# A graph network of six message passes: edge groups without holes, and consumers that walk pairs of group and tile

## The chip, the cores and the metric

The kernel runs on one core of a Trainium2 chip. The metric is the device time of one execution in microseconds (us). Three runs of the kernel before gave a median of 14,485.1 us, from 14,473.6 to 14,488.4. The core's engines have instruction queues of their own: TensorE (PE, its weight loads PEld), VectorE (DVE), ScalarE (ACT), GpSimd (POOL) and SyncE (SP). They meet through semaphores.

## The reference

There are 6,250 nodes with 64 features and 200,000 edges (src, dst), sorted by dst, with a weight, 16 attributes and 8 attributes each. After a layer norm and a ReLU each of four blocks adds its result to x:

```
L0: 3 times  agg[dst] += weight * ht[src]            (hyperbolic layers, 64 features)
L1: e = leaky_relu(er[dst] + el[src] + attributes16 . v);  softmax of e over the edges of a dst;
    h[dst] += alpha * xt[src];  then a layer norm
L2: h[dst] += relu(A[src] + B[dst] + attributes8 @ E) @ W2
L3: as L1, without attributes, with another slope
```

These are six passes over all edges: three GCN passes (n = 0, 1, 2), attention (n = 3), MLP (n = 4), attention (n = 5).

## The kernel before

**Groups and tiles.** The nodes are T = 49 tiles of 128. A group is 256 edges, two columns of 128, and all edges of a group point into one tile. The kernel sorts the edges itself: it counts them by tile, gives each tile a whole number of groups (the last one of a tile has holes), and computes where each edge goes. The number of groups must hold for any distribution, so NG = 832, in ITER = 52 iterations of BODY = 16 groups. A table `sched` gives the tile of each group; it goes through DRAM into one partition, and PE and DVE load 24 of its words into registers at the head of each iteration (`tiles_of`).

**Before the passes.** DVE computes positions in chunks (`PLACED`), SP brings slabs of the payload, and POOL scatters them with 1,568 indirect DMAs (line 450) into `packed` in DRAM, 32 words an edge. `packed` has been filled with harmless values before that, by 42 DMAs of SP. Then SP reads `packed` back, 16 columns at a time in two buffers, and DVE unpacks them (`unpack`, line 1167) into W, DL, SRC, EAV and EA8. Three iterations are unpacked ahead, the others within the first pass.

**A pass.** A node table goes to DRAM. SP copies 16 indices at a time from SRC to `idx`; POOL gathers the rows of the source nodes, one indirect DMA for a column of 128 edges (line 469), into G, which has room for 16 groups. A gather of group q waits until group q of the iteration before is used. Semaphores are one for each place q in the ring, and consumers wait for `gathered[..][q]` (`need_rows`). In a GCN pass only 28 of 32 columns come so; the last four are chosen on PE from a copy of the table on the chip: DVE makes one-hots of each of the 49 tiles (`tile_hots`, line 788), PE multiplies (line 1559), DVE takes the sums into G (`take_rows`). The MLP pass does that for two columns, attention for none.

**The consumers** go through the groups in order. GCN: DVE makes a weighted one-hot of the destinations (line 749), PE multiplies it with G (line 1534), DVE adds the result to ACC at the group's tile (line 924). Attention is a chain of some 13 small DVE instructions a group (own scores line 768, maximum 838 to 845, shift 859 to 865, exponents 873 to 881, one-hot 760, weighing 887, adding up 930), with transposes and products on PE and one-hots and exponentials on ACT. MLP: line 896 adds the gathered row to what PE computed, then ReLU and a split in three bf16 parts, line 927 adds up. All loops over iterations are hardware loops whose bodies are unrolled over the 16 groups; each engine walks its own in program order.

Of the kernel before, what the change touches and what calls it, by code (L numbers as in the profile page):

```python
# [23 lines left out]
P = 128  # L24
# [13 lines left out]
NG = -(-((N_EDGES + T * (GE - 1)) // GE) // BODY) * BODY  # L38
PLACED = [2, 3, 5, 9, 15, 15]
ACT_BINS = 28  # L40
PACK = 40
NS = 1680
# [4 lines left out]
ROW = D + 1  # L47
ITER = NG // BODY
PASSES = 6
PIECE = BODY  # L50
AHEAD = 3
# [13 lines left out]

assert STEPS_N % 2 == 1 and 2 * ITER * PIECE == 2 * NG
assert max(PLACED) * 2 * SLAB <= 512 and sum(PLACED) * 2 * SLAB == KC and NS % PACK == 0 and (NS // PACK) % 2 == 0 and KC % (2 * SLAB) == 0
assert NS * P >= NG * GE + P * KC - N_EDGES + GE and P * SCHED >= NG + BODY

# [33 lines left out]
def build(nc, d, out):  # L103
    with ExitStack() as ctx:
# [17 lines left out]
        W = sb("W", [P, NS])  # L122
        DL = sb("DL", [P, NS])
        SRC = sb("SRC", [P, 2 * NG + 2 * BODY], I32)
        EAV = sb("EAV", [P, NS])
        EA8 = sb("EA8", [P, NS, D8])

        ea8_flat = EA8[:, :, :].rearrange("p s c -> p (s c)")
        bucket, mask, signs, rank = (ea8_flat[:, i * KC:(i + 1) * KC] for i in range(4))
        signs = signs.bitcast(BF16).rearrange("p (h c) -> p h c", h=2)  # L130
        dst_raw = ea8_flat[:, 5 * KC:6 * KC].bitcast(I32)
        pos = ea8_flat[:, 6 * KC:7 * KC].bitcast(I32)
        pos_hi = ea8_flat[:, 7 * KC:8 * KC].bitcast(I32)
# [8 lines left out]
        fill = y_flat[:, 0:PACK * PAY].rearrange("p (s c) -> p s c", c=PAY)  # L142
        slab = y_flat[:, PACK * PAY:PACK * PAY + 2 * SLAB * PAY].rearrange("p (h s c) -> p h s c", h=2, c=PAY)
# [4 lines left out]
        grp_i = sb("grp_i", [P, NB], I32)  # L148
        sums = sb("sums", [P, NB])
        before = U[:, :, :].rearrange("p t c -> p (t c)")[:, 0:SCHED * T].rearrange("p (j t) -> p j t", t=T)  # L150
        sched_f = sb("sched_f", [P, SCHED])
        sched_i = sb("sched_i", [P, SCHED], I32)
        sched = sb("sched", [1, P * SCHED + LAG], I32)
# [35 lines left out]
        G = sb("G", [P, 2 * BODY, ROW])  # L189
# [73 lines left out]
        packed = nc.dram_tensor("packed", (P, NS, PAY), F32).ap()  # L263
        packed_rows = packed.rearrange("p s c -> (p s) c")
        table = nc.dram_tensor("table", (P * TP, ROW), F32).ap()
        sched_d = nc.dram_tensor("sched_d", (P * SCHED,), I32).ap()
# [4 lines left out]
        fill_made, filled = sem("fill_made"), sem("filled")  # L271
# [48 lines left out]
        def landed(n):  # L320

            return 32 * ITER * LANDS[:n].count(LANDS[n])
# [5 lines left out]
        def steps(eng, body, lag):  # L328


            for u in range(BODY):
                body(u, 0)
            with nc.Fori(1, ITER, engines=[eng.engine], hint_back_edge=True) as i:
                body(None, i)
            for u in range(lag):
                body(u, ITER)
# [8 lines left out]
        def _(sp):  # L345
# [20 lines left out]
            sp.wait_ge(fill_made, 1)  # L366
# [5 lines left out]
            sp.wait_ge(fill_made, 2)  # L372
            for k in range(NS // PACK):
                sp.dma_start(packed[:, k * PACK:(k + 1) * PACK, :], fill).then_inc(filled, 16)

            sp.wait_ge(sched_made, 2)
            sp.dma_start(sched_d.rearrange("(p j) -> p j", p=P), sched_i[:, :]).then_inc(sched_stored, 16)
            sp.wait_ge(sched_stored, 16)
            sp.dma_start(sched[0:1, LAG:LAG + P * SCHED], sched_d.rearrange("(a n) -> a n", a=1)).then_inc(sched_loaded, 16)
# [14 lines left out]
            for h in range(2):  # L394
                sp.wait_ge(scattered[h], KC // (2 * SLAB) * 16 * SLAB)
            sp.wait_ge(first_rows, 1)

            def fetch(j):

                for h in range(2):  # L400
                    if not isinstance(j, int) or j > 0:
                        sp.wait_ge(unpacked, j * 2 + h)
                    sp.dma_start(pack_buf[h], packed[:, ds((j * 2 + h) * PIECE, PIECE), :]).then_inc(pack_in[h], 16)
# [1397 lines left out]
```

## Time and profile before

The profiled execution of the kernel before has a span of 14,473.0 us from its first to its last instruction; the median of the runs, 14,485.1 us, is 12.1 us above it.

| | PE | PEld | DVE | ACT | POOL |
|---|---|---|---|---|---|
| busy, us | 9,746.3 | 8,816.7 | 10,317.1 | 5,084.8 | 10,529.2 |
| share of the span | 67% | 61% | 71% | 35% | 73% |

The chain of waits that ended last goes by engine: PE 39%, issue 18%, DVE 16%, POOL 14%, DVE's queue 8%, ACT 3%, DMA 2%. The first 2,213 us are setup and scatters. The passes then take, from one boundary to the next, about 1,895, 1,875, 1,858, 2,166, 2,012 and 2,121 us.

An engine's busy time is what its instructions cover; instructions of a queue alone (register operations, waits, loads of registers) are shown as DVEq, PEq, SPq and are not in it. "Issue" is time for which the profile shows no wait. In a list of one line's instructions the three durations are minimum, median and maximum in ns, then come the first and the last start.

### The profile page before, as it was taken

To read this page: it belongs to the slowest core of one execution; us is meant where nothing else is said; L and a number is where in the kernel's file an instruction comes from. 1 tells how busy PE (TensorE), PEld (TensorE's weight loads), DVE (VectorE), ACT (ScalarE), POOL (GpSimd) and SP (SyncE) were. 2 spreads that over 40 slices of the span, in tenths; PEclk is the share of its full clock that TensorE was granted. 3 is DMA by queue.
4 is the path that set the end of the run, shared out by engine and by line. 5 is a ranking of instruction groups with operands and counts; after the bars stand their busy time and mean duration, and the time that the engine had idled before them with its cause. 6 is when DMAs were issued, how large, how long until landed. Compare 5 with 4: busy or idle time off the path is not lost.

```text
span 14473.0 us, 400585 instructions
## 1 busy us (share of the span) xinstructions
PE 9746.3 (67%) x94470; PEld 8816.7 (61%) x94471; DVE 10317.1 (71%) x47961; ACT 5084.8 (35%) x16333; POOL 10529.2 (73%) x10828
## 2 busy tenths in 40 slices
PE   0000006777778888788887788888577777888888
PEld 0000006777767777677777677777455555777777
DVE  7870007777776666666666888888888887888888
ACT  1000000000000000000000788888577676777777
POOL 3777777777767777677777677777577776677776
PEclk9995557888888888888888555555788888555555
DMA  2101112222211111111111111111111111111111
GB/s 101 26 25 26 26 26 47 41 41 41 40 27 27 27 27 27 27 27 27 27 27 25 30 28 27 27 27 27 23 26 26 26 26 24 30 28 28 28 28 30
DMA packets 496417, 441.99 MB, mean 31 GB/s; under 512 B 289869, under 2 KB 315085, under 8 KB 494926
## 3 DMA queue, kind: packets, MB, share of 16 engines
q0 software_dynamic: 346368, 334.42, 13.9%
q1 hardware_dynamic: 149454, 102.38, 2.5%
q14 instruction: 556, 4.55, 0.1%
q8 instruction: 39, 0.64, 0.0%
HBM read 364.93 MB, written 65.20 MB: 30 GB/s over the span
## 4 chain that ended last, share of the span: by engine, by line
PE 39%; issue 18%; DVE 16%; POOL 14%; DVEq 8%; ACT 3%; DMA 2%; ACTq 0%; POOLq 0%; SPq 0%
PE bank L1559 16%; PE bank L1534 11%; POOL packed L450 9%; POOL G L469 4%; DVEq L732 4%; PE bank L1616 3%; PE bank L1628 3%; DMA G<-table,idx 2%; DVE OH L749 2%; PE bank L1605 1%; PE bank L1718 1%; PE bank L1547 1%; DVEq L734 1%; PE bank L1632 1%; DVE OHT L788 1%
## 5 line engine op out<-in xcount | busy, mean ns | idle before, releaser
L469 POOL DMA_INDIRECT G<-table,idx x9256 | 9007.0, 973 | 3237.1 <-issue 2497.9
L1452 ACT ACTIVATE OHB<-bank,const 128x512 bf16<-128x512 f32 x159 | 109.2, 687 | 6718.5 <-PE bank L1547 6718.5
L1559 PE MATMUL bank<-UZ,OHT 128*128 128x192 bf16 x15600 | 2093.5, 261 | 543.5 <-DVE OHT L788 543.5
L1534 PE MATMUL bank<-G,OH 128*128 128x64 f32 x9984 | 1683.9, 300 | 589.0 <-DVE OH L749 449.6
L450 POOL DMA_INDIRECT packed<-Y,slab_pos x1568 | 1522.0, 971 | 671.5 <-issue 495.4
L1559 PE MATMUL bank<-UZ,V 128*128 128x192 bf16 x14976 | 1994.0, 259 | 0.0
L1534 PEld LDWEIGHTS bank<-G,OH 128*128 128x128 f32 x9984 | 1494.1, 217 | 760.2 <-DVE OH L749 678.6
L1559 PEld LDWEIGHTS bank<-UZ,OHT 128*128 128x128 bf16 x15600 | 1511.1, 111 | 583.0 <-DVE OHT L788 561.4
L1534 PE MATMUL bank<-ZR,OH 128*128 128x65 f32 x6656 | 1765.4, 419 | 1.8 <-DVE ZR L887 1.8
L1534 PEld LDWEIGHTS bank<-ZR,OH 128*128 128x128 f32 x6656 | 1623.8, 334 | 2.1 <-DVE ZR L887 2.0
L749 DVE TENSOR_SCALAR OH<-const,DL,W 128x128 f32<-128x128 f32 x4992 | 1560.6, 367 | 0.2 <-issue 0.2
L924 DVE TENSOR_TENSOR ACC<-ACC,bank 128x64 f32 x2496 | 550.0, 220 | 1241.4 <-PE bank L1534 1203.9
L788 DVE TENSOR_SCALAR OHT<-OHB 128x512 bf16<-128x512 bf16 x3900 | 1157.7, 297 | 388.1 <-issue 386.8
L1559 PEld LDWEIGHTS bank<-UZ,V 128*128 128x128 bf16 x14976 | 1408.1, 104 | 16.0
L1628 PE MATMUL bank<-ER,OHT 128*128 x9984 | 1001.4, 174 | 505.0 <-DVE negm_lo L865 310.4
L1628 PEld LDWEIGHTS bank<-ER,OHT 128*128 128x128 bf16 x9984 | 783.8, 105 | 786.8 <-issue 617.8
L1616 PE MATMUL bank<-const,V 128*128 128x128 f32 x3328 | 1117.9, 440 | 57.7 <-ACT V L1391 49.9
L788 DVE TENSOR_SCALAR V<-OHB 128x512 bf16<-128x512 bf16 x3744 | 1143.5, 305 | 0.0
L1547 PE MATMUL bank<-const,chosen 128*128 128x128 f32 x1272 | 222.6, 330 | 1293.1 <-DVE chosen L524 1293.1
L760 DVE TENSOR_TENSOR OHB<-iota_b,DLw 128x256 bf16<-128x256 bf16 x2496 | 1046.8, 419 | 21.6 <-issue 12.6
L1547 PEld LDWEIGHTS bank<-const,chosen 128*128 128x128 f32 x1272 | 195.5, 233 | 1293.7 <-DVE chosen L524 1293.7
L1605 PE MATMUL bank<-ident_b,OHB 128*128 128x128 bf16 x4992 | 942.9, 286 | 19.0 <-DVE OHB L760 19.0
(303 smaller groups left out, 21034.3 us busy)
## 6 DMA issues: line engine op xcount, KB each, us to landing
G<-table,idx POOLq DMA_INDIRECT x9256, 2.5
packed<-Y SPq DMA_DIRECT2D x42, 640.0 KB, 17.7
UZ<-packed SPq DMA_DIRECT2D x104, 256.0 KB, 2.7
Y<-in_payload SPq DMA_DIRECT2D x98, 256.0 KB
packed<-Y,slab_pos POOLq DMA_INDIRECT x1568
table<-Y SPq DMA_DIRECT2D x6, 1690.0 KB, 5.5
idx<-SRC SPq DMA_DIRECT2D x624, 8.0 KB
X<-in_x SPq DMA_DIRECT2D x1, 1568.0 KB, 8.0
```

The lines of the kernel that those rows point to most:

```text
L450: pool.indirect_dma_start(out=packed_rows, out_offset=bass.IndirectOffsetOnAxis(ap=slab_pos[:, h, c:c + 1], axis=0), in_=slab[:, h, c, :], ...
L469: pool.indirect_dma_start(out=G[:, 2 * q + c, :], out_offset=None, in_=table, in_offset=bass.IndirectOffsetOnAxis(ap=idx[:, h, j:j + 1], a ...
L732: v.load(tregs, sched[0:1, bass.ds(i * BODY, BODY + LAG)] if not isinstance(i, int) else sched[0:1, i * BODY:(i + 1) * BODY + LAG])
L749: o = v.tensor_scalar(OH[:, q, c, :], iota, DL[:, at], W[:, at], ALU.is_equal, ALU.mult)
L760: v.tensor_tensor(OHB[:, q, :, :], iota_b[:, :].unsqueeze(1).to_broadcast([P, 2, P]), DLw[:, 2 * u:2 * u + 2].unsqueeze(2).to_broadcast([P ...
L788: v.tensor_scalar(tile_hot(tile), code, float(tile), None, ALU.is_equal).then_inc(tile_ready, 1)
L1534: o = pe.matmul(ps_a[r % 2][:, 0:w], OH[:, q, c, :], parts[c], start=c == 0, stop=c == 1)
L1547: o = pe.matmul(ps_code[:, c * P:(c + 1) * P], chosen[:, c:c + 1].to_broadcast([P, P]), ident, start=True, stop=True)
L1559: o = pe.matmul(ps_rows[c // 2][:, c % 2 * 3 * D:(c % 2 + 1) * 3 * D], tile_hot(tile)[:, c * P:(c + 1) * P], table_parts[:, tile, :, :].re ...
L1605: o = pe.matmul(ps_m[r % 2][:, c * P:(c + 1) * P], OHB[:, q, c, :], ident_b[:, :], start=True, stop=True)
L1616: o = pe.transpose(ps_x[r % 2][:, c * P:(c + 1) * P], V[:, r % 4, c, :], ident)
L1628: pe.matmul(e[:, c:c + 1], one, ER3[:, bass.ds(t, 1), k], start=k == 0, stop=k == 2)
```

## The change

The edges are packed without holes. Group g is edges 256 g to 256 g + 255 of the order by dst, so there are NGR = 784 groups in NCH = 49 iterations of gathers. A group may now touch several tiles. The consumers walk a list of *pairs* (group, tile); there can be 782 + 48 of them, and the list is still NG = 832 long, ITER = 52 iterations. For an edge of another tile than the pair's the local destination lies outside 0..127: no one-hot matches it, and a mask adds a very low score in attention. The table `sched` has four rows (tile, group, first pair of a group, and tile and column together); `quads` holds the group of each fourth pair. G is a ring of RING = 4 iterations, 64 groups, and POOL's loop is unrolled over the four.

Consumers no longer wait on the semaphore of a place. SP waits for each gather in order and counts `rows_here`; a consumer waits every fourth pair until `rows_here` has reached the group of a pair some steps on, a value that it has in a register. The column in G comes out of a register too. The fill of `packed` is gone; `packed` is read back by pairs, each a DMA of two columns, on ACT's queue in the first pass; the 8 attributes go through a table in DRAM (`e8_items`) and come back in the MLP pass; the indices are brought from the order of pairs to that of groups by 16 DMAs an iteration. The table-row work on the chip is done in the first 49 iterations alone.

```diff
+NGR = KC // 2
+NCH = NGR // BODY
-NG = -(-((N_EDGES + T * (GE - 1)) // GE) // BODY) * BODY
+NG = -(-(-(-N_EDGES // GE) + T - 1) // BODY) * BODY
+RING = 4
-AHEAD = 3
+AHEAD = 5
...
+        def values(eng, what, n, top):
+            loads[0] += 1
+            regs = [eng.alloc_register(f"v{loads[0]}_{j}") for j in range(n)]
+            eng.load(regs, what)
+            return [eng.snap(r, donate=True, min_val=0, max_val=top) for r in regs]
+        def items_of(eng, row, i, back, top):
+            return values(eng, sched[0:1, row, ds(i * BODY + (LAG - back), BODY + back)], BODY + back, top)
+        def quads_of(eng, i):
+            return values(eng, quads[0:1, ds(i * (BODY // 4), BODY // 4 + 1)], BODY // 4 + 1, NGR - 1)
+        def need_rows(eng, n, quad, u, i):
+            if u % 4 == 2 or (u == 0 and isinstance(i, int)):
+                eng.wait_ge(rows_here, (quad[(u + 2) // 4 if u else 0] & 1023) + (n * NGR + 1))
...
+                def rows_of(i, last):                                  # SP, in each pass
+                    for h in range(2):
+                        end = min(BODY // 2 * (h + 1), fetched(n))
+                        for q in range(BODY // 2 * h, end):
+                            sp.wait_ge(gathered[LANDS[n]][q], i * 32 + (landed(n) + 32))
+                            sp.sem_inc(rows_here, 1)
+                        if not last:
+                            indices(i + 1, h)
+                    for q in range(fetched(n), BODY):
+                        ...
+                        sp.sem_inc(rows_here, 1)
...
-                gathers(0)
-                with pool.Fori(1, ITER) as i:
-                    gathers(i)
+                gathers(0, 0)
+                with pool.Fori(0, NCH // RING) as i:
+                    for k in range(RING):
+                        gathers(i * RING + (k + 1), (k + 1) % RING)
...
-                    need_rows(g, q)
-                    v.tensor_tensor(EL[:, r, :], G[:, 2 * q:2 * q + 2, D], EAV[:, bass.ds(g * 2, 2)],
+                    need_rows(v, n, quad, u, i)
+                    v.tensor_tensor(EL[:, r, :], G[:, bass.ds(col, 2), D], (EAV if n == 3 else MASK)[:, ds(g * 2, 2)],
...
-                    v.tensor_tensor(ZR[:, r % 4, :, 0:D], G[:, 2 * q:2 * q + 2, 0:D],
+                    v.tensor_tensor(ZR[:, r % 4, :, 0:D], G_wide[:, bass.ds(col, 2), 0:D],
...
-                        if live(0) and n == 3:
-                            own_scores(g, u, u % 8)
+                        if live(0):
+                            own_scores(g, u, i, u % 8, cols[u + LAG], quad)
...
-                        sums(g, u % 8, u % 2, n, [G[:, 2 * u + c, 0:D] for c in range(2)], D)
+                        sums(g, u % 8, u % 2, n, [G[:, bass.ds(body.cols[u] + c, 1), 0:D].rearrange("p a c -> p (a c)")
+                                                  for c in range(2)], D)
...
+                    own.count(v.tensor_scalar(MASK[:, at], DL[:, at], 0.0, None, ALU.is_lt))      # in unpack
+                    stt(MASK[:, at], DL[:, at], float(P - 1), MASK[:, at], ALU.is_gt, ALU.add)
+                    ts(MASK[:, at], MASK[:, at], NO_SCORE, None, ALU.mult)
+                    tt(EAV[:, at], EAV[:, at], MASK[:, at], ALU.add)
...
+                def each(i, fetching):                                 # ACT, in the first pass
+                    a.wait_ge(unpacked, (i + AHEAD) * 2 + 3)
+                    if fetching:
+                        fetch(i + AHEAD + 1)                           # 16 DMAs of two columns
+                    to_groups(i + 2)                                   # 16 DMAs of SRCI to SRC
+                    code_made(0, i + 1)
+                    if fetching:
+                        store_e8(i + AHEAD + 1)                        # 2 DMAs
```

## Rows read from the trace of the kernel before

**Rows 1.** Windows of four passes: length, then PE, PEld, DVE, ACT, POOL busy.

```profile
4155.00:6030.00 1875.00, 1539.00 (x14040) 1448.98 (x14040) 1258.33 (x5205) 47.80 (x104) 1411.77 (x1451) 0.85 0.17 26
...
7995.00:10161.00 2166.00, 1862.44 (x16640) 1649.14 (x16640) 1784.30 (x10923) 1764.94 (x5826) 1595.01 (x1664) 0.50 0.17 28
...
10265.00:12277.00 2012.00, 1457.59 (x18616) 1161.53 (x18616) 1628.61 (x8319) 1415.57 (x4211) 1532.23 (x1551) 0.82 0.16 26
...
12330.00:14451.00 2121.00, 1847.09 (x16640) 1660.38 (x16640) 1788.01 (x10091) 1660.80 (x5825) 1596.80 (x1664) 0.50 0.17 28
```

**Rows 2.** The gathers, line 469, in the windows of passes 1, 3, 4, 5.

```profile
L469 POOL DMA_INDIRECT G<-table,idx x1451: 940/944/1381, 4154.8 to 6007.7; - x182
...
L469 POOL DMA_INDIRECT G<-table,idx x1664: 938/944/1197, 8000.6 to 10127.3; - x185
...
L469 POOL DMA_INDIRECT G<-table,idx x1551: 940/944/1493, 10265.0 to 12268.6; - x194
...
L469 POOL DMA_INDIRECT G<-table,idx x1664: 940/944/1196, 12334.4 to 14437.1; - x185
```

**Rows 3.** Timeline of POOL in pass 1: start, duration, idle before.

```profile
5012.53 0.94 POOL L469 DMA_INDIRECT G<-table,idx  x1 [0.30 <-issue]
```

**Rows 4.** DVE once a group: line 924 in pass 0, line 873 in 3, 5.

```profile
L924 DVEq FUSED_REGOPS  x832: 57/65/70, 2238.0 to 4091.6; - x167
...
L873 DVE TENSOR_TENSOR e_u<-EL,bank x832: 142/149/158, 8014.5 to 10157.8; 128x2 f32<-128x2 f32 x167
L873 DVE TENSOR_TENSOR e_u<-G,bank x832: 142/149/158, 12345.5 to 14447.6; 128x2 f32<-128x2 f32 x167
```

**Rows 5.** Timeline of DVE in pass 3, one step.

```profile
9002.18 0.15 DVE L873 TENSOR_TENSOR e_u<-EL,bank 128x2 f32<-128x2 f32 x1
...
9004.38 0.15 DVE L873 TENSOR_TENSOR e_u<-EL,bank 128x2 f32<-128x2 f32 x1
```

**Rows 6.** Timeline of DVE in pass 0, one half of an unpack.

```profile
3015.74 0.18 DVE L524 TENSOR_SCALAR W<-UZ 128x16 f32 x1 [0.36 <-issue]
...
3017.22 0.16 DVE L1184 TENSOR_SCALAR itmp<-UZ 128x16 int32<-128x16 int32 x1
3017.51 0.18 DVE L1187 SCALAR_TENSOR_TENSOR SRC<-itmp 128x16 int32 x1
3017.83 0.17 DVE L524 TENSOR_SCALAR W<-UZ 128x16 f32 x1
```

**Rows 7.** Chain of waits at the head of an iteration, pass 1: start, us.

```profile
5011.13 1.60 DVEq L732
...
5012.76 0.23 DVEq L734
...
5013.02 0.17 DVEq L734
```

**Rows 8.** Chain of waits in pass 3, within one step.

```profile
9003.18 0.04 DVEq L864
...
9003.48 0.23 issue
...
9004.07 0.08 DVEq L768
```

**Rows 9.** Timeline of PE in pass 1: one sum to the next.

```profile
5023.06 0.58 PE L1534 MATMUL bank<-G,OH 128*128 128x64 f32 x4
...
5024.80 0.58 PE L1534 MATMUL bank<-G,OH 128*128 128x64 f32 x4
```

**Rows 10.** Timeline of POOL: the first scatter and the first gather.

```profile
157.41 1.12 POOL L450 DMA_INDIRECT packed<-Y,slab_pos  x1 [156.95 <-DMA slab_pos<-EA]
...
2220.47 1.44 POOL L469 DMA_INDIRECT G<-table,idx  x1 [26.56 <-DMA idx<-SRC]
```

**Rows 11.** Timeline of SP: two DMAs of a slab.

```profile
1503.09 0.34 SPq L391 DMA_DIRECT2D Y<-in_payload  x1
1503.57 0.50 SPq L392 DMA_DIRECT2D slab_pos<-EA  x1
```

More of the change, by code:

```diff
@@ L47 @@
 ROW = D + 1
+RING = 4
+COLS = RING * 2 * BODY
 ITER = NG // BODY
@@ L392, in _ @@
                         sp.dma_start(slab_pos[:, h, :], pos[:, bass.ds(at, SLAB)]).then_inc(slab_in[h], 16)
[L394 to L403, printed above, removed]
-            for j in range(AHEAD):
-                fetch(j)
-            sp.wait_ge(unpacked, 2 * AHEAD + 1)
             for n in range(PASSES):
@@ L1441, in body @@
                                 tiles(i + 1, 0)
+                a.wait_ge(quads_made, 1)
+                for h in range(2):
+                    a.wait_ge(e8_out[h], 16 * ITER)
+                load_e8(0)
                 codes(0)
                 tiles(0, 0)
-                steps(a, body, 1)
-            def codes(n):
-                def made(i):
-                    a.wait_ge(code_spread, i + (n * (ITER + 1) + 1))
-                    need(a, tile_ready, i * T + n * ITER * T)
-                    a.activation(code, ps_code[:, 0:ON_CHIP * P], ACT.Identity, bias=own_row).then_inc(code_ready, 1)
-                made(0)
-                with a.Fori(1, ITER + 1) as i:
-                    made(i)
+                for u in range(BODY):
+                    body(u, 0, True)
@@ new lines, in mlp_pass, with code_made @@
+                with nc.Fori(1, NCH, engines=[a.engine], hint_back_edge=True) as i:
+                    body(None, i, True)
+                with nc.Fori(NCH, ITER - 1, engines=[a.engine], hint_back_edge=True) as i:
+                    body(None, i, False)
+                for u in range(BODY):
+                    body(u, ITER - 1, False, last=True)
+                body(0, ITER, False, last=True)
+            def code_made(n, i):
+                a.wait_ge(code_spread, i + (n * (NCH + 1) + 1))
+                need(a, tile_ready, i * T + n * NCH * T)
+                a.activation(code, ps_code[:, 0:ON_CHIP * P], ACT.Identity, bias=own_row).then_inc(code_ready, 1)
@@ L1722, in mlp_pass @@
                 spread_e(0)
-                steps(pe, with_tiles(step), 6)
+                steps(pe, with_tiles(step), 6, on_chip=True)
             pe.wait_ge(sched_loaded, 16)
-            tregs = [pe.alloc_register(f"tile{j}") for j in range(BODY + LAG)]
             pe.wait_ge(blocks_made, 2)
```

485 lines of the change are left out of this document (291 added, 194 removed).

## The prediction

> **What bounds the kernel now.** I read the table by stretch first, because six passes, n = 0 to 5, with different limits fill 12,200 of the 14,473 us. [rows 1]: GCN passes of about 1,870 us (n = 1 is shown), attention passes of 2,166 and 2,121 us, the MLP pass of 2,012 us. In each the engine with the most regular work is POOL, which issues the gathers. Its list of starts [rows 2] gives the pace: 1,456 gathers (1,451 recorded) in 1,853 us in pass 1, 1.273 us each, so 28 x 1.273 = 35.7 us an iteration; 30 gathers in 38.6 us in the MLP pass; 32 in 40.9 and 40.5 us in the attention passes. The median gather takes 0.944 us, and 0.30 us of issue lie before the next [rows 3]; a few longer ones make up the rest, so in GCN and MLP the queue of gathers never rests: it is the bound, though the chain of waits mostly names PE and DVE.
>
> Next the pace of the consumers [rows 4]: 16 groups take 16/831 of the time from first to last. That is 35.7 us in pass 0, 41.3 and 40.5 in the attention passes. In attention I then read single steps of DVE [rows 5]: from one e_u to the next is 2.20 us in the middle of an iteration, and in it the instructions start one behind the other without a gap. 16 such steps and the head of an iteration, with its table load, are the 41.3 us. So attention has two bounds within 1%: POOL and DVE. Fewer gathers can lower only one of them. PE is third: at a granted clock of 0.50 it is busy 1,862 of 2,166 us [rows 1], 35.8 of 41.7 an iteration.
>
> **The arithmetic of the change.** The edges are 200,000/256 = 782 groups, padded to 784 = 49 iterations; before, they were 832 = 52. But the list of pairs has 782 + 48 = 830 entries, padded to 832. So the gathers, and the choice of rows from the on-chip table, drop by 3 iterations of 52 a pass; every step of the consumers (one-hots, sums, scores, adding up) is still made 832 times, and now finds its column by a register.
>
> **Step 1, GCN passes 1 and 2.** Removed: 3 x 35.7 = 107 us of gathers a pass. What is late next: the consumers. Groups arrive for 49 x 35.7 us and must serve 52 iterations of pairs, so the consumers have 33.6 us for 16 pairs. What they need can be read from pass 0, where DVE also unpacks two halves of 2.1 us [rows 6] and hardly waits: 35.7 - 4.2 = 31.5 us, at most. The change adds on DVE a load of 5 registers and four waits on a register's value. The load of 24 takes 1.60 us and the two copies behind it 0.23 + 0.17 [rows 7]. Between those ends, one fifth of 1.60 (0.33) and 1.60, I take 0.95; the copies go, as the registers are now donated: +0.5 net. A wait with its register instruction is 0.04 to 0.08 and 0.05 before the next [rows 8]: 4 x 0.15 = 0.6, half of it hidden where PE paces at 1.74 us a pair [rows 9]. PE must compute two addresses a pair: 0 (run ahead, behind 16 matmuls) to 0.2 us (both bare), so 0 to 3.2 us an iteration; I take 0.9. Its new load of 16 registers lies beside DVE's, during which PE waits. In all 31.5 + 0.5 + 0.3 + 0.9 = 33.2 us, just under 33.6. I take -100 us for each pass, -200, with -107 and -20 as ends of one.
>
> The Trainium skill (DMA: Bandwidth & Descriptors, Latency and other measured facts) gives a register load a floor of about 600 ns; an estimate by it, 0.6 plus 5/24 of the remaining 1.0, is 0.8 us instead of my 0.95, which would change an attention pass by 8 us. No run shows a short load yet.
>
> **Step 2, the MLP pass.** 3 x 38.6 = 116 us of gathers go. DVE, busy 1,629 of 2,012 us [rows 1] or 31.3 an iteration, keeps POOL's pace now; it gains the 0.4 us of copies and pays a column for `hidden`, 16 x 0.1 = 1.6 us, on a need that I put near 35 us (31.3 and the 3.7 that a head of an iteration takes without work). The wait for rows goes to ACT, which is busy 1,416 of 2,012 us [rows 1]; behind it queue the transposed one-hots, and ACT also issues one 64 KB load of attributes an iteration. Taken: -108 (ends -116 and -40).
>
> **Step 3, attention.** No gather that is saved helps, since DVE sets 41.3 us. Queued behind its new wait, in own_scores, is its whole instruction stream; V on ACT and the shift wait for that. Added per pair: own_scores and weigh address G by a register (decode, multiply, base), the tile number is decoded twice, and one wait in four pairs. The chain shows the address of EAV in one fused register instruction, 0.08 us, between L841 and L768, bare [rows 8]; two or three more operations there cost about 0.05. The window of 0.23 us before ZR (behind the reduction L838) hides weigh's. Decoding the tile adds about 0.02. Sum 0.08 us a pair; ends 0 (all hidden) and 0.35 (four register instructions of 0.04 with their 0.05, all bare). So 16 x 0.08 = 1.3, +0.5 load, +0.6 waits, -0.3 of waiting for rows that goes: 2.1 us, times 52 = +109 us (ends +20 and +330) for pass 3. Pass 5 had no own_scores: the two differ by 41.3 - 40.5 = 0.8 us an iteration. 0.8 + 2.1 = 2.9 us, and the pace before was 40.5: +151 us (ends +60 and +370).
>
> A rule that speaks for this price: the Trainium skill (Vector Engine (DVE) Microarchitecture Reference, Instruction fetch and dispatch) says that every DVE instruction passes through the full dispatch, register instructions too. The trace agrees in so far as these take 0.04 to 0.08 us of DVE's queue each [rows 8], with 0.05 to the next.
>
> **Step 4, before and in pass 0.** The schedule needs some 25 more small DVE operations ahead of the first positions, on the path to the first scatter at 157.4 us [rows 10]: about +8, less 1 for the fill that goes. The fill's writes are over long before and return nothing. The start: now POOL rests 26.6 us between the last scatter and the first gather at 2,220.5 [rows 10]. Now ACT must fetch by groups, 16 DMAs where there were 2. One on SP took 0.34 us, with a register on an SBUF side 0.50 [rows 11]; ends on ACT 0.3 and 1.0, taken 0.5. A round is 16 issues, 8 us, and some 4 us of landing and of the first half of an unpack, 12 us; SRC of the first iteration needs the fourth round and 16 more DMAs, so gathers start near 2,263. DVE's further unpacks lie in that wait: consumers start 39 us later. The iteration: unpack has 12 operations a half, not 9, three or four of them dependent, 0.29 us from one to the next (L1184 to L1187) [rows 6]: +1.9. With the half microsecond of load, 0.2 of waits and 0.5 for PE, less 0.9 of waiting for rows: 35.7 + 2.2 = 37.9 us. 47 x 37.9 + 2 x 33 + 3 x 20 (no table rows) = 1,907 against 1,856: +51. Pass and start +90 (ends -60 and +220). ACT's queue then holds 34 DMAs, about 25 us of 38, so the code it also makes is in time.
>
> **Sum.** 7 + 90 - 200 - 108 + 109 + 151 = +49 us on the profiled execution's 14,473.0, which becomes 14,522. The median of the runs, 14,485.1, lies 12 us above that span; so 14,535 us.
>
> **The rivals.**
> A, the queue has room: DVE's register work is hidden and the load is short. Attention +25 and +65, MLP -112, GCN -107 each, pass 0 with its start +50, setup +7: -179 us, 14,306. For it: gaps of 0.23 us in the step; against it: only one such gap in 2.20 us.
> B, decoding is not fused: four bare register instructions a pair, 0.35 us. Attention +310 and +350, pass 0 +180, MLP -50, GCN -50 each, +7: +697, 15,182. Also a halfway case. Against it: the address of EAV is one fused instruction, 0.08 us.
> C, pass 0 becomes bound by ACT: 34 DMAs at 1.0 us and the register loads make about 43 us, and the code for the table rows, queued behind them, comes late. From 0.75 us a DMA this decides. 46 x 5 = +230 over my sum, 14,765. By the Trainium skill (DMA: Bandwidth & Descriptors, Specifications) pieces under 512 B are not moved at line rate; here they are 256, 32 and 8 B. That would lengthen landings, of which five iterations of lead hide 100 us.
> D, the consumers in GCN need over 34.4 us for 16 pairs, PE's addresses bare: GCN gains 20, not 100: +160, 14,695.
>
> **How the numbers follow.** Forecast 0.45, A 0.27, B (with its halfway case) 0.10, C 0.08, D 0.10. The range 14,300 to 14,830 holds A, the forecast, C and D, and leaves out some 2 in 10; the forecast's own is 14,440 to 14,640. Runs of this kernel tell about 0.2%, 29 us, from no change. Faster is A and a tenth of chance out of the forecast's lower end: 0.36; same 0.14; slower 0.50.
>
> **What would show it.** 1,372 gathers in passes 1 and 2, at 1.27 us, and these passes near 1,770 us; DVE waiting for rows seldom there. Attention: e_u to e_u in mid-iteration 2.25 to 2.30 us, 43.4 us an iteration in both passes, POOL with gaps over 0.30 us. The short TENSOR_LOAD near 0.95 us. Pass 0: heads of iterations 2 us longer, ACT DMAs near 0.5 us, first gather near 2,270. I am wrong if attention's step stays at 2.20 us (A), if it goes beyond 2.4 (B), or if pass 0 has DVE waiting on ACT's code (C).

## The result: 2.8% slower, and where the time went

The kernel after the change takes 14,897.6 us (median of 4 runs, 14,886.2 to 14,902.6), the kernel before 14,486.8 us (4 runs, 14,473.6 to 14,494.9): a ratio of 1.028, interval 1.0267 to 1.0296. The prediction, 14,535 with 14,300 to 14,830 as its range, is too low by 363 us. Slower was right; the size of one step, attention, was not, and pass 0 had the wrong sign.

In the profiled execution (span 14,884.4 us, of before 14,473.0) I took the stretches one after the other, each from its first to its last add-up of a sum, and set them beside the terms of the prediction:

```
stretch                           before    after   change   predicted
up to the first add-up of n = 0   2238.2   2331.9    +93.7   +7 and (with the pass) +90
n = 0, GCN                        1853.5   1802.0    -51.5
n = 1, GCN                        1854.6   1751.6   -103.0   -100
n = 2, GCN                        1854.6   1757.8    -96.8   -100
n = 3, attention                  2138.7   2403.2   +264.5   +109
n = 4, MLP                        1994.9   1874.5   -120.4   -108
n = 5, attention                  2096.4   2503.3   +406.9   +151
between passes, end                                  +18         0
```

The windows of the same four passes as in [rows 1] (length, then PE, PEld, DVE, ACT, POOL busy, PEclk), the answer of the kernel after:

```profile
4200.00:5956.00 1756.00, 1391.34 (x13324) 1351.88 (x13323) 1207.15 (x5039) 34.05 (x50) 1327.55 (x1365) 0.85 0.17 26
7870.00:10278.00 2408.00, 1897.17 (x16570) 1646.53 (x16570) 1854.65 (x10874) 1690.97 (x5799) 1461.64 (x1547) 0.50 0.14 23
10394.00:12273.00 1879.00, 1426.67 (x18232) 1141.63 (x18231) 1628.05 (x8200) 1353.43 (x4038) 1421.88 (x1451) 0.84 0.18 30
12356.00:14865.00 2509.00, 1889.98 (x16562) 1653.44 (x16562) 1946.18 (x10877) 1691.21 (x5793) 1461.21 (x1546) 0.50 0.13 22
```

Pass 3 is 242 us longer than in [rows 1], and DVE's busy time in it grew by only 70: what was added is not vector work. The gathers, answering to [rows 2], by pass (count, durations, first and last start):

```profile
L518 POOL DMA_INDIRECT scratch<-table,idx x1372: 940/944/3357, 4186.9 to 5942.3; - x196
L518 POOL DMA_INDIRECT scratch<-table,idx x1568: 938/944/1146, 7843.2 to 10096.1; - x196
L518 POOL DMA_INDIRECT scratch<-table,idx x1470: 940/945/4784, 10355.6 to 12256.8; - x184
L518 POOL DMA_INDIRECT scratch<-table,idx x1568: 938/942/1187, 12328.3 to 14674.9; - x196
```

In GCN and MLP one starts every 1.28 and 1.29 us, as before, and there are 84 and 90 fewer: the gain is their number. In attention one starts every 1.44 and 1.50 us: POOL waits now, and the last add-up comes 180 and 187 us after the last gather. The group's step on DVE, as in [rows 4] and [rows 5]: e_u by pass, then from one e_u to the next.

```profile
L935 DVE TENSOR_TENSOR e_u<-EL,bank x830: 142/149/158, 7865.9 to 10266.5; 128x2 f32<-128x2 f32 x166
L935 DVE TENSOR_TENSOR e_u<-EL,bank x832: 142/149/158, 12348.8 to 14857.5; 128x2 f32<-128x2 f32 x167
```

```profile
9018.63 0.15 DVE L935 TENSOR_TENSOR e_u<-EL,bank 128x2 f32<-128x2 f32 x1
9021.11 0.15 DVE L935 TENSOR_TENSOR e_u<-EL,bank 128x2 f32<-128x2 f32 x1
```

A plain step (by that I mean the length from one e_u to the next that stands most often in the pass) takes 2.48 us where it took 2.20; in pass 5 it is 2.63 where it was 2.16, and the median of all its steps is 2.79. The chain of waits through own_scores shows what came in, where [rows 8] had one fused instruction of 0.08 us:

```profile
9015.18 0.04 DVEq L836
9015.22 0.03 issue
9015.26 0.10 DVEq L836
9015.36 0.03 issue
9015.39 0.05 DVEq L836
9015.44 0.05 issue
9015.49 0.07 DVE EL L836
```

The first is the mask that takes the column out of the register (ALU_OP), the other two are the addresses of G and of EAV (FUSED_REGOPS). So a mask is an instruction of its own; so is each address; and each has an issue of 0.03 to 0.08 us behind it. The same holds at the sums: the line of add_up has now two register instructions a pair, where it had one fused one of 0.064:

```profile
L991 DVEq ALU_OP  x1664: 40/45/50, 7872.2 to 14862.0; - x185
L991 DVEq FUSED_REGOPS  x1664: 98/106/113, 7872.2 to 14862.1; - x185
```

The loads (the short one had no row before; [rows 7] had the long one and its copies, which are gone):

```profile
L384 DVEq TENSOR_LOAD <-sched x318: 1598/1604/1864, 2317.0 to 14846.8; - x159
L384 DVEq TENSOR_LOAD <-quads x260: 590/595/616, 2318.9 to 14801.0; - x130
L384 ACTq TENSOR_LOAD <-quads x52: 534/538/562, 10378.2 to 12226.3; - x52
```

And the start, answering to [rows 10]: the first scatter, the last scatters, the first gather on POOL.

```profile
177.29 1.12 POOL L499 DMA_INDIRECT packed<-Y,slab_pos  x1 [176.83 <-DMA slab_pos<-scratch]
...
2226.41 0.96 POOL L499 DMA_INDIRECT packed<-Y,slab_pos  x1 [0.31 <-issue]
2305.31 0.97 POOL L518 DMA_INDIRECT scratch<-table,idx  x1 [77.94 <-DMA idx<-SRC]
```

### The profile page after: what moved, and what is told of

Read it like the earlier page. It is cut to its first block, busy times and chain, and to the rows that moved or that the text cites. A ratio compares the mean times of both kernels' runs of the same rounds, so it can differ in the third digit from the quotient of the medians.

```text
span 14884.4 us, 423582 instructions
## 1 busy us (share of the span) xinstructions
PE 9489.7 (64%) x92328; PEld 8592.3 (58%) x92329; DVE 10563.2 (71%) x48623; ACT 5003.6 (34%) x16178; POOL 10002.6 (67%) x10294
## 4 chain that ended last, share of the span: by engine, by line
issue 23%; PE 22%; POOL 19%; DVE 18%; DVEq 11%; ACT 4%; DMA 2%; ACTq 1%; POOLq 0%; SPq 0%
PE bank L1720 11%; POOL packed L499 10%; POOL scratch L518 9%; PE bank L1698 5%; DVEq L384 4%; DVE ZR L949 2%; DMA scratch<-table,idx 2%; DVEq L836 2%; DVE OHB L828 1%; DVE negm_lo L927 1%; PE bank L1771 1%; PE bank L1783 1%; PE bank L1873 1%; DVE r_rest L924 1%; ACT OHT L1440 1%
## 5 line engine op out<-in xcount | busy, mean ns | idle before, releaser
L518 POOL DMA_INDIRECT scratch<-table,idx x8722 | 8466.6, 971 | 3981.8 <-issue 2525.2
L1720 PE MATMUL bank<-UZ,OHT 128*128 128x192 bf16 x14700 | 1979.2, 262 | 702.1 <-DVE OHT L858 702.1
L1698 PE MATMUL bank<-scratch,OH 128*128 x9984 | 1638.1, 295 | 521.5 <-DVE ACC L985 322.7
L1720 PE MATMUL bank<-UZ,V 128*128 128x192 bf16 x14112 | 1890.2, 260 | 0.0
L1720 PEld LDWEIGHTS bank<-UZ,OHT 128*128 128x128 bf16 x14700 | 1429.6, 111 | 738.6 <-DVE OHT L858 715.8
L1698 PEld LDWEIGHTS bank<-scratch,OH 128*128 128x128 f32 x9984 | 1476.8, 214 | 581.6 <-issue 570.6
L1720 PEld LDWEIGHTS bank<-UZ,V 128*128 128x128 bf16 x14112 | 1332.7, 105 | 15.9
L1466 ACT ACTIVATE V<-OHB,EL 128x128 f32<-128x128 bf16 x3328 | 1153.4, 393 | 518.0 <-DVE EL L836 415.3
L858 DVE TENSOR_SCALAR V<-OHB 128x512 bf16<-128x512 bf16 x3528 | 1058.3, 300 | 0.0
L1708 PE MATMUL bank<-const,chosen 128*128 128x128 f32 x1200 | 170.9, 286 | 1295.4 <-DVE chosen L574 1295.4
```

What stands on the lines that cost most here:

```text
L518: pool.indirect_dma_start(out=G[:, slot * 2 * BODY + 2 * q + c, :], out_offset=None, in_=table, in_offset=bass.IndirectOffsetOnAxis(ap=idx ...
L858: v.tensor_scalar(tile_hot(tile), code, float(tile), None, ALU.is_equal).then_inc(tile_ready, 1)
L1466: o = a.activation(V[:, r % 4, c, :], OHB[:, q, c, :], ACT.Identity, scale=-BIG, bias=EL[:, r, c:c + 1])
L1698: o = pe.matmul(ps_a[r % 2][:, 0:w], OH[:, q, c, :], parts[c], start=c == 0, stop=c == 1)
L1720: o = pe.matmul(ps_rows[c // 2][:, c % 2 * 3 * D:(c % 2 + 1) * 3 * D], tile_hot(tile)[:, c * P:(c + 1) * P], table_parts[:, tile, :, :].re ...
```

## The experiments

The theory after the result (T): attention pays for register instructions in DVE's queue. Against it stood: a cost of the packed layout itself, waiting for the count of arrived groups, and register work that lies hidden. A place is the number of an instruction in the iteration. Times are medians; the interval is that of the ratio to the kernel before, run beside it on the same chip.

**pairs_in_attention.** Everything of the change stays in GCN and MLP; attention gathers by pairs again.

```
- sp: idx <- SRC (by groups), NCH rounds
+ sp, n in (3, 5): idx <- SRCI (by pairs), ITER rounds; pool: G[:, 2q + c, :], fixed
- G[:, bass.ds(col, 2), ...]; need_rows out of quads; own_scores in both passes
+ G[:, 2 * q:2 * q + 2, ...]; wait_ge(gathered[1][u], i * 32 + ...); own_scores in n = 3 only
```

> The changed kernel, but both attention passes (n = 3, 5) gather by pairs again: 832 x 2 gathers with fixed columns of G out of the unpacked list SRCI, no table of columns, no waits out of a table, no own_scores in pass 5 (its scores are read straight from G as before). GCN and MLP stay packed. The theory (T): the loss of attention is register work in VectorE's queue, so pass 3 goes from 2,403 back to about 2,140 us (first to last add-up) and pass 5 from 2,503 to about 2,095, while passes 0, 1, 2 and 4 keep 1,802, 1,752, 1,758 and 1,875: 14,898 - 264 - 407 = about 14,225 us, a ratio to the kernel before of 0.982. The rival (R): the loss comes with the packed layout itself (G inside the large scratch tile, a ring of 64 groups, lists changed) or with the boundaries, and then attention stays over 2,250 us a pass and the kernel over 14,480.

Measured: 14,171.5 us, ratio 0.979 (0.9772 to 0.9805), faster than both. e_u in the two passes:

```profile
L966 DVE TENSOR_TENSOR e_u<-EL,bank x832: 142/149/158, 7861.6 to 9968.8; 128x2 f32<-128x2 f32 x167
L966 DVE TENSOR_TENSOR e_u<-scratch,bank x832: 142/149/159, 12043.5 to 14139.2; 128x2 f32<-128x2 f32 x167
```

Pass 3 takes 2,102 us from first to last add-up, pass 5 2,093, with G still inside the large tile: the layout costs nothing that shows, and the whole loss of attention belongs to how consumers find and await their rows and tiles and, in pass 5, to own_scores, which went too. Pass 3 is even 37 us shorter than before; the reason comes below. These 37, and 16 us less between the passes, make up the 54 by which the kernel is under my 14,225.

**before_one_mask.** In the kernel before, add_up masks its tile's register.

```
+ if att: t = t & 63
  acc = ACC[:, bass.ds(t, 1), :]
```

> The kernel before, with one more register instruction a pair on VectorE in both attention passes: add_up masks the register of its tile (t & 63, which changes nothing) ahead of the address. The price of one bare register instruction. T: 0.04 and 0.05 to the next, 0.09 us x 832 x 2 = +150 us at most, 14,635, ratio 1.010; less where part of it falls into a stall of the step. Rival A: 0. As fused in the prediction's step 3 (0.02 a pair): +33 us, ratio 1.002.

Measured: 14,569.8 us, ratio 1.006 (1.0047 to 1.0081), +90 us. That lies between the 150 of T and the 33 of fused work, but it is no price of a mask: in pass 3 a plain step went from 2.21 to 2.25 and the pass became shorter, 2,100 us, while pass 5 took 2,217 (+120), with steps of 2.24 instead of 2.16. The chain at the head of an iteration of pass 5 has what the sum did not (the branch is line 333):

```profile
12507.60 0.07 DVEq L333
12507.66 2.05 issue
12509.71 0.04 DVEq L333
```

The same place in pass 5 of the kernel before:

```profile
12534.88 0.07 DVEq L333
12534.95 0.46 issue
12535.41 0.04 DVEq L333
```

1.6 us an iteration, 84 us a pass, behind the branch, where nothing was changed but the 16 more instructions in each attention loop. This gave theory L, the position of the code.

**before_addresses.** Meant to add the addresses of G as well.

```
+ col = v.snap(t & 64, min_val=0, max_val=1) + 2 * q     # in weigh and own_scores
```

> The kernel before, with the register work of the change added to VectorE in both attention passes and nothing else of it: weigh and (in pass 3) own_scores find their column of G by a register (one mask of the tile's register, which gives 0, and the address from it), add_up masks its tile. Same gathers, same waits, same results. T: pass 3 gains 0.25 us a pair (three masks of 0.04 with their 0.05, not all of the address hidden), 0.20 to 0.28: 832 x 0.25 = +208; pass 5, without own_scores, 0.17 (0.09 to 0.20): +141; together +350 us, 14,835, ratio 1.024. The rival (A as in the prediction: register work is hidden in the gaps of the step): under +50 us, ratio under 1.004.

Measured: 14,560.8 us, ratio 1.0055 (1.0038 to 1.0071). Its trace has the same instructions as before_one_mask: the address, being 0 by its bounds, was folded away. It is a second measurement of one mask, and says nothing on the addresses.

**wait_by_pair.** No table for the wait.

```
- if u % 4 == 2 ...: eng.wait_ge(rows_here, (quad[...] & 1023) + (n * NGR + 1))
+ if PLAN[n][0] == ATT and u % 4 == 0: eng.wait_ge(rows_here, i * BODY + (n * NGR + u + 4))
```

> The changed kernel, in attention only the wait for rows is changed: every fourth pair waits on the count of arrived groups against a value made of the loop's counter (16 i + u + 4), later than needed, instead of one out of the table; the load of 5 registers and the masks of that value go. T: an iteration loses the 0.6 us of the short load and of four times 0.36 us some 0.23 each, 1.5 us in all, 52 x 1.5 = 78 us a pass, 14,898 - 156 = about 14,740 us. The rival (W, consumers really wait for arrivals, counted by SP): waiting for a group up to 48 groups later than the one needed makes the passes longer, over 14,950 us. If neither the load nor the masks are on the path: 14,900.

Measured: 14,912.3 us, ratio 1.0299 (1.0282 to 1.0316). Pass 3 fell from 2,403 to 2,353 us, pass 5 rose from 2,503 to 2,573: its gap behind the branch is 2.3 us where the kernel after has 0.52. Without that (1.8 x 52 = 94) pass 5 would be 24 us shorter. The total stands where I had put it for a load and masks that are not on the path (14,900), but by two changes that cancel. The rival W fails: pass 3 became shorter though it waits for later groups. The register work of the wait costs 1.0 us an iteration in pass 3, less than the 1.5 expected. The steps of 3.02 us that held the wait are gone from pass 3, but some of 2.82 to 2.88 stand there, about 0.36 above the plain 2.49: by the size, gaps of the kind that pairs_shifted shows below.

**static_columns, twice.** The addresses of G go. Own_scores and weigh read fixed rows of Y in their place, so this kernel leaves the gathered rows out of attention's sums; gathers, waits and masks of the tile stay.

```
- G[:, bass.ds(col, 2), D]                 (own_scores)
+ Y[:, 2 * u:2 * u + 2, D]
- G_wide[:, bass.ds(col, 2), 0:D]          (weigh)
+ Y[:, 2 * r:2 * r + 2, 0:D]
```

> The changed kernel, in attention only: own_scores and weigh read two fixed rows of Y (the table's source, not written during a pass) instead of the two columns of G that a register names. It leaves the gathered rows out of attention's arithmetic; gathers, waits, masks of the tile and everything else stay. It prices the addresses of G. The theory in its present form (N: attention pays per instruction put into VectorE's queue, about 0.058 us each, 5.09 us an iteration for 86 instructions in pass 3 and 7.84 for 135 in pass 5): four register instructions and one fused one go from the step, so the step falls from 2.49 to about 2.30 us in pass 3 and from 2.55-2.63 to about 2.40 in pass 5; 16 x 0.2 = 3.2 us an iteration, 166 us a pass, about 14,570 us, give or take 90 us for the code's position (theory L below). Rival (the addresses lie hidden beside vector work, and the masks of the tile and the waits are the price): under 0.05 us a pair, over 14,820 us.

This run, pairs_shifted and early_start fell on a chip on which the kernel before takes 19,835 us, not 14,480. They gave 19,952 (ratio 1.005, 1.003 to 1.007), 20,020 (1.009, 1.0066 to 1.0106) and 19,982 us (1.008, 1.006 to 1.0093): on that chip packing GCN and MLP shows no gain either. I had put its state down to PE standing still; in its trace of static_columns PE does so for up to 4.3 us between 11,300 and 11,420 us, but in the same stretch of the second time for up to 4.8, so that is not what sets the chip apart. What does stays open. All three were run again on another.

> The kernel static_columns once more, on another chip. The first time the kernel before itself took 19,835 us, and the trace of this kernel shows PE standing still for 2 to 3.7 us some twice in 145 of its instructions (11,300 to 11,420 us) and 28 gathers in 47 us: a state of that chip in which attention is bound by PE's stream, so that its ratio, 1.005, says nothing on VectorE's. Expected on a chip where the kernel before takes 14,480 us, as written then: N 14,570 us (step of pass 3 at 2.30 us, of pass 5 at 2.40), 90 us either way for the code's position; rival over 14,820 us with steps within 0.05 us of 2.49 and 2.63.

Measured: 14,583.0 us, ratio 1.0075 (1.0058 to 1.0092). e_u by pass:

```profile
L935 DVE TENSOR_TENSOR e_u<-EL,bank x832: 142/149/158, 7869.5 to 10121.7; 128x2 f32<-128x2 f32 x167
L935 DVE TENSOR_TENSOR e_u<-EL,bank x832: 142/149/158, 12197.6 to 14560.0; 128x2 f32<-128x2 f32 x167
```

A plain step takes 2.28 us in pass 3 and 2.44 in pass 5 (expected 2.30 and 2.40; the medians of all steps are 2.45 and 2.61), the passes are 156 and 146 us shorter, the kernel 315. The addresses of G are three fifths of attention's loss in pass 3, a third in pass 5; the rival (hidden addresses) is out. In the chain above it is own_scores' address that stands bare; weigh's mask and address (L949, 0.045 and 0.057 us) run beside a reduction of 0.42 us.

**pairs_own_scores.** pairs_in_attention, but with the masked scores kept in pass 5, on fixed columns.

```
- if live(0) and n == 3: own_scores(...)
+ if live(0): own_scores(...)        # EL = G[..., D] + (EAV if n == 3 else MASK)
```

> The kernel pairs_in_attention with own_scores kept in pass 5, as the change has it, on fixed columns of G (the mask of foreign edges added to the scores; in pairs_in_attention these scores go in unmasked and their weights meet zeros of the one-hots). It prices that operation alone: one vector instruction and two to three register and semaphore instructions a pair. At 0.058 us an instruction: 4 x 0.058 = 0.23 us, 3.7 us an iteration, +190 us at most; as pass 3 had it before (2.21 against 2.16 us a step): +0.05 us, +42 us. I take +60 to +120: 14,230 to 14,290. Rival (0.19 us of pass 5's 0.47 are own_scores, by the difference of the passes' losses): +158, 14,330.

Measured: 14,312.6 us, ratio 0.989 (0.9873 to 0.9906). Pass 5 takes 2,230 us, +138, its plain step 2.34 instead of 2.16; its branch's gap is 0.92 us instead of 0.53, 20 us of the 138. The rival's 0.19 us a step was right, my 60 to 120 too low.

**pairs_shifted, twice.** Code moved, nothing else.

```
+ if att:
+     for _ in range(64): v.wait_ge(s_const, 16)    # compiled to 32 instructions, once a pass
  steps(v, body, lag, ...)
```

> The kernel pairs_in_attention (14,171 us) with nothing but 32 more instructions on VectorE ahead of each attention loop (waits on a semaphore that has long its value), executed once a pass: they move the loops' code by 32 instructions in pass 3 and 64 in pass 5. Theory L (position of code): the traces show an extra gap of 0.36 us on VectorE every 128 instructions, seen or hidden beside a long instruction, and after the loop's branch 0.27, 0.52, 2.16 or 2.34 us in different kernels. If position decides these, the visible gaps of pass 3 move from places 47 and 175 of the iteration to 15 and 143, those of pass 5 from 10, 138, 266 to 74, 202, 330, and a pass changes by -60 to +100 us. Rival (they belong to the instructions that stand there): both passes as before, 2,102 and 2,092 us, within 10 us.

> The kernel pairs_shifted once more, on another chip (the first time 20,020 us against 19,835 of before, bound by PE's gaps; VectorE's visible extra gaps of pass 3 had moved from places 47 and 175 to 143 and 271 of the iteration, its gap behind the branch stayed 0.53 us). Expected: gaps of 0.36 us at 15, 143 and 271 of pass 3, at 74, 202 and 330 of pass 5 unless hidden; total 14,110 to 14,270. Rival (no effect of position): 14,171 within 15 us and gaps at the old places.

Measured, the second time: 14,211.0 us, ratio 0.982 (0.9802 to 0.9835), 40 more than pairs_in_attention (on another chip, on which the kernel before takes 5 us less). Pass 3 is unchanged in length (2,105), its visible gaps have moved from places 47 and 175 to 143 and 271; pass 5 takes 2,145 us, +53, and its branch shows:

```profile
12223.66 0.07 DVEq L356
12223.73 2.37 issue
12226.09 0.04 DVEq L356
```

In pairs_in_attention that issue is 0.46. L holds: behind the branch the same instructions take 1.9 us an iteration more 64 places further on. Of these 99 us a pass only 53 show, for pass 5 had been held by POOL before (below), and DVE had slack. The other part of L is seen inside an iteration, here of pass 5 of pairs_in_attention (chain, place 266):

```profile
12256.73 0.04 DVE e_u L966
12256.77 0.41 issue
12257.18 0.05 DVEq L90
```

At that place of every iteration, and at 10, 138 and 394, such a gap stands, 128 instructions apart; elsewhere the issue is mostly 0.03 to 0.08. Some fall beside a long instruction and are hidden, others add 0.36 us to a step.

**early_start, twice.** pairs_in_attention with another order at the start.

```
- the pair list ahead of the first positions        + after the fourth stretch of them
- act: store_e8(3), fetch(4), to_groups(0)          + to_groups(0), store_e8(3), fetch(4)
- act: fetch(5), to_groups(1), code_made(0, 0)      + fetch(5), code_made(0, 0), to_groups(1)
- dve: unpack(1..4), three_parts                    + three_parts, unpack(1..4)
```

> The kernel pairs_in_attention (14,171 us) with the start in another order and nothing less done: the pair list is computed after the fourth stretch of positions and not ahead of the first, ScalarE issues the 16 copies of SRC's first iteration ahead of the fifth round of fetches, and the code for the table's rows ahead of the second 16 copies; the three parts of the table are made while the first fetches are on their way. What pass 0 lost in the change is 94 us to the first add-up: 20 at the first scatter (2 before it, 6 for the pair list, 12 in heads of the loop over the bins), 13 of slower scatters, and some 60 from the last scatter to the first add-up. Theory: 8 us of it return at the first scatter, 12 at the first gather, 12 to 20 more at the first add-up (ScalarE's code is waited for): 30 to 40 us, about 14,135 us. Rival (DVE's unpack halves are the chain, the rounds overlap anyway): under 10 us.

> The kernel early_start once more, on another chip (the first time 19,982 us against 19,835 of before). Expected as then: first scatter 8 us earlier (177 to 169), first gather 12 us nearer to the last scatter, first add-up 24 to 40 us earlier, about 14,135 us. Rival: under 10 us, over 14,160.

Measured, the second time: 14,151.1 us, ratio 0.978 (0.976 to 0.9793), 20 us under pairs_in_attention, not 35. The two ran on different chips and their intervals overlap; in the traces the first add-up comes 18 us earlier. Its POOL at the same places:

```profile
158.33 1.12 POOL L526 DMA_INDIRECT packed<-Y,slab_pos  x1 [157.87 <-DMA slab_pos<-scratch]
...
2212.12 0.96 POOL L526 DMA_INDIRECT packed<-Y,slab_pos  x1 [0.30 <-issue]
2284.01 0.97 POOL L545 DMA_INDIRECT scratch<-table,idx  x1 [70.94 <-DMA idx<-SRC]
```

The first scatter comes 19 us earlier than in the kernel after, the last one 14. 8 of the 19 are the list; 10 are the loop over the bins, which has the same instructions but takes 1.84 us a turn again and not 2.05, 49 times (position once more, I think; no run moved this loop alone). From last scatter to first gather only 7 us are won; that the first rounds now wait for the table's parts on DVE is read from the order of the edit, not measured.

Over all kernels, what one iteration of attention takes (the pass over 52), beside the instructions that DVE executes in it and the median time from its branch to its next instruction. The last two columns are counts for the whole pass: packets of 8 KB of the queue q14, kind "instruction", and how often POOL stood over 0.4 us between two gathers (all worked out from the traces):

```
kernel                 pass   instructions   us an iteration   behind the branch   code packets   POOL rests
pairs_in_attention     5      468            40.3              0.53                261            0
before                 5      471            40.4              0.53                261            0
pairs_in_attention     3      486            40.5              0.53                258            0
before_one_mask        5      487            42.7              2.14                260            85
before                 3      489            41.2              0.52                260            39
before_one_mask        3      505            40.4              0.27                9              0
static_columns_2       3      511            43.3              0.52                261            57
pairs_own_scores       5      517            43.0              0.92                260            101
static_columns_2       5      542            45.4              0.52                262            206
wait_by_pair           3      569            45.3              0.52                262            253
after                  3      575            46.3              0.52                262            363
wait_by_pair           5      600            49.5              2.29                311            641
after                  5      606            48.2              0.52                263            657
```

From before to after: 86 more instructions and 5.1 us in pass 3, 135 and 7.8 in pass 5: 0.059 and 0.058 us each. Single kernels lie up to 1.8 us off such a line, and 505 instructions ran faster than 489. The last two columns explain most of that.

*POOL's pace.* Where POOL never rests, a pass takes what its gathers take, 32 x 1.26 = 40.4 us an iteration, and DVE's need lies somewhere below. That holds for the four passes at 40.3 to 40.5. Pass 3 before stood over it, by 0.8 us, and so the 37 us that pairs_in_attention gained there are the way down to POOL's pace. What DVE's 3 fewer instructions and their position did for it is not shown apart. POOL's waits for DVE in the middle of pass 3, of the kernel before (8,040 to 10,120 us) and of pairs_in_attention (7,890 to 9,950; us in all, times, longest):

```profile
POOL G L469 <- DVE ZR L887: 120.7, 319, 1.6
...
POOL scratch L545 <- DVE ZR L980: 67.7, 222, 0.3
```

The price of 0.058 in pass 5 is thus a lower bound; the 0.059 of pass 3 starts from a pass in which POOL waited for DVE.

*Loading of code.* In attention 5 packets of 8 KB come each iteration, in wait_by_pair's pass 5 six. In pairs_in_attention and pairs_shifted_2 one starts 0.8 to 1.1 us after the beginning of each place where such a gap stands or hides, 128 instructions apart, and the packets moved with these places. Where the branch is followed by 2.1 us or more, a packet starts 0.1 to 0.6 us behind it and DVE goes on 1.8 to 2.0 us later; in the kernels with 0.53 the first one starts 1.15 us behind the branch, when DVE has gone on. In pass 3 of before_one_mask almost none comes, no gap of that kind stands in the loop and 0.27 us stand behind the branch, as in the GCN passes (3 to 9 packets a pass). The queue in the kernel before (8,040 to 10,120 us) and in before_one_mask (8,040 to 10,100; packets, MB, share of 16 DMA engines):

```profile
q14 instruction: 253, 2.07, 0.3%
...
q14 instruction: 5, 0.04, 0.0%
```

So position acts by when, and whether, the loop's code is loaded again. The trace doesn't name the engine for which a packet comes; that these are DVE's follows from their moving with an edit of DVE's code alone. Which loops keep their code I can't say from these runs: one of 505 instructions did, one of 468 did not.

## Why the prediction was wrong, step by step

**What bounds the kernel.** Right for passes 1 to 5: POOL in GCN and MLP, POOL and DVE close together in attention (DVE by 0.8 us an iteration in pass 3, POOL in pass 5). For pass 0 it was wrong to say that DVE hardly waits: in the kernel before it stood 272.7 us, 5 an iteration, before its add-ups for PE.

**Step 1, GCN.** Right: -103 and -97 against -100 each, gathers at 1.28 us; rival D (consumers over 34.4 us) did not come. **Step 2, MLP.** -120 against -108: POOL's whole gain, 3 x 38.6 = 116, arrived, and the 8 us that I had held back for consumers were not paid.

**Step 3, attention, is the step that failed**, by "Sum 0.08 us a pair". Measured is 0.28 us a plain step in pass 3 and 0.47 in pass 5. I took the decoding to be fused into the address, as EAV's is. It isn't: every mask is an instruction of its own beside the fused one (L836 and L991 above, and L949), own_scores has three register instructions in a row before it, and of the two addresses only weigh's is hidden, as I said. The nearest forecast was rival B, at 0.10: in attention its mechanism is what happened and its size nearly too (+265 and +407 against its +310 and +350), and of the signs announced "beyond 2.4" came. That the whole came out near its halfway case and not at 15,182 is another matter: B also had pass 0 lose 180 us and GCN and MLP gain only 50 each, and there it failed. The upper end of my step, 0.35 a pair, was in the working; the value was chosen by the one row that looked alike. For pass 5 I took own_scores at 0.8 us an iteration, the difference of two passes before; pairs_own_scores measures 2.7 (of which 0.4 are the branch's gap), and it starts from POOL's pace, so the need grew by at least that. Pass 5 before stood at POOL's pace, 40.4, and I took that for DVE's need; so the difference of the two passes was no price. Of the smaller terms the short load is 0.595 us, not 0.95 (by the Trainium skill's floor of about 600 ns, DMA: Bandwidth & Descriptors, Latency and other measured facts: on DVE the trace agrees with 0.595, on ACT 5 registers took 0.538), so the head of an iteration paid 0.2 us net and not 0.5.

**Step 4, start and pass 0.** Together +42 against +97, by two errors that cancel. Setup: the first scatter came 20 us later, not 7: the list 6 (8 forecast), 12 in the loop over the bins (49 turns of 2.05 us, 1.81 before, with the same instructions), 2 ahead of the list. The scatters themselves took 979 ns in the mean instead of 971, 1,568 of them, 13 us; no run tells why. From last scatter to first add-up it is 105 us where it was 45: a fifth round of fetches stood in ACT's queue ahead of the copies for SRC, and DVE's first one-hots waited for a code that ACT makes behind 36 more DMAs; I had stopped at the fourth round and the gather. An ACT DMA took 0.34 us (fetch) and 0.52 (SRC), so 0.5 was near, and rival C (ACT the bound) did not come:

```profile
L1568 ACTq DMA_DIRECT2D UZ<-packed x832: 334/339/1132, 2230.1 to 3947.3; - x167
...
L1582 ACTq DMA_DIRECT2D SRC<-scratch x800: 514/517/1622, 2290.0 to 4012.7; - x160
```

The iteration of pass 0 takes 35.8 us in the mean, not 37.9: DVE's 1.7 us of further unpacking went into its slack (it waits 172.2 us for PE before its add-ups, where it waited 272.7), and POOL, with 28 gathers at 1.28 us, still sets it. So pass 0 gained 52 us where I had it lose 51.

**What was not in the prediction at all** is the position of code and its loading. It did not make this result (both attention loops have 5 code packets an iteration before and after, and the same 0.52 us behind the branch), but it decided the sign of single experiments, up to 94 us a pass. The Trainium skill (Runtime: NRT & Kernel Launch, Instruction fetch mechanics) says that a taken branch to a block that isn't held forces a fetch before going on; the gaps of 2.05 and 2.37 us behind the branch, against 0.46, agree, with a packet of code starting inside them. It also says that sequential fetch is hidden by the rate of issue, in blocks of 256 instructions; here gaps of 0.36 us stand every 128, and not all are hidden.

## What to carry to other kernels

Where an engine is within 1% of being the bound, count the instructions that a change puts into its queue, register instructions too, and price each: here 0.06 us, hidden only where the trace shows a gap of that size in front of the very instruction. A saving that belongs to one engine should be taken only in the stages that this engine bounds: the same packing, left out of attention, turned +2.8% into -2.1%. Before a difference of 1% between two loops is given a cause, look at the gap behind their branches and count the code packets in the loop; and before a small change is priced, see whether another engine already holds the loop, for then part of the price is not seen.

## What the runs showed of the hardware

On DVE one register instruction costs 0.04 to 0.11 us and an issue of 0.03 to 0.08, about 0.06 net. A load takes 0.595 us for 5 registers and 1.60 for 24 on DVE, 0.538 for 5 and 1.02 for 16 on ACT: 0.33 and 0.053 a register on DVE. In attention loops of 468 to 606 instructions on DVE, 5 (once 6) packets of 8 KB of code came each iteration, and a gap of about 0.36 us stood every 128 instructions; in one loop of 505 instructions almost no packet came and no such gap stood. From a loop's branch to DVE's next instruction it was 0.27, 0.53, 0.92, 2.1 or 2.4 us, by position alone where 32 instructions were put ahead of the loops (0.53 to 2.4). And one chip ran the unchanged kernel 37% slower; why stays open.
